# A graph network on one core: the feature block's place in the sum passes, and one signal of TensorE for both

## What is computed

```python
# layer 0, three times:
neigh_mean = segment_sum(h[dst], src, num_segments=n) * inv_deg[:, None]
out = elu(h @ Wg + deg_pos[:, None] * (neigh_mean @ Wl + h @ Ws) + b)
# x = layernorm(x + layer 0)
# layer 1, over the edges in both directions and a loop at each node:
source_node_vec = segment_sum(concat(x[node_i], stf)) / count
neighbors_sum = relu(segment_sum(concat(x[node_j], ef, et) @ W1.T + b1, node_i))
out = concat(neighbors_sum, source_node_vec) @ W2.T + b2
# x = layernorm(x + layer 1)
```

## Time and profile before

| | us |
|---|---|
| median of 3 runs | 10882.93 (10874.25 to 10888.81) |
| the profiled execution | 10844.11 |
| its span | 10842.3 |
| DVE busy | 6451.6 (60%) |
| PE busy, matmuls | 7015.7 (65%) |
| POOL busy | 5221.8 (48%) |
| ACT busy | 3571.9 (33%) |
| sum passes together | 3366 |

### The profile page before, as it was taken

The page is one execution under the profiler, slowest core; times in us unless marked ns, Lnnn a source line. Parts: engine busy times, 40 slices in busy tenths (PEclk is TensorE's granted clock), DMA queues, the critical chain, the costliest instruction groups (busy, mean ns, idle before and its releaser), DMA issues.

```text
span 10842.3 us, 191817 instructions
## 1 busy us (share of the span) xinstructions
PE 7015.7 (65%) x46640; PEld 5921.0 (55%) x46640; DVE 6451.6 (60%) x15194; ACT 3571.9 (33%) x10119; POOL 5221.8 (48%) x4833
## 2 busy tenths in 40 slices
PE   7899981167009999655576665766645566666666
PEld 6688871167008888544444555445544455445556
DVE  8899980022016666544586556865567655675556
ACT  0133320000007777433394112931128511491111
POOL 0058886778654444566304662046620366306660
PEclk9999999999999999777698777987769877897776
DMA  9965555555559999665497665976648866896671
GB/s 385 389 192 143 146 143 139 142 127 126 133 137 308 305 304 301 202 168 166 90 376 269 197 198 111 377 251 195 198 83 338 287 197 197 243 392 193 196 188 28
DMA packets 1567388, 2320.61 MB, mean 214 GB/s; under 512 B 974516, under 2 KB 1046056, under 8 KB 1567320
## 3 DMA queue, kind: packets, MB, share of 16 engines
q1 hardware_dynamic: 1227608, 1356.73, 37.3%
q0 software_dynamic: 292608, 911.36, 30.7%
q10 hardware_dynamic: 47104, 51.75, 2.0%
HBM read 1328.55 MB, written 986.78 MB: 214 GB/s over the span
## 4 chain that ended last, share of the span: by engine, by line
issue 25%; PE 24%; another core or an unknown queue 16%; DVE 14%; ACT 8%; DMA 7%; DVEq 3%; POOL 2%; ACTq 2%; SPq 1%; POOLq 0%
PE ps L759 9%; PE ps L736 4%; DVE mask L1310 3%; ACT ring L1075 3%; PE ps L836 3%; ACT hring L1085 3%; DMA frows<-by_src 2%; PE ps L752 2%; DMA gathered<-ring 2%; DVE ohj L1228 2%; DVE prod L1294 2%; PE ps L747 1%; POOL ring L634 1%; PE ps L674 1%
## 5 line engine op out<-in xcount | busy, mean ns | idle before, releaser
L650 POOL DMA_INDIRECT ring<-gathered,gidx x2176 | 2190.3, 1007 | 3096.1 <-DMA gathered<-ring 1978.2
L580 POOL DMA_INDIRECT by_src<-prow,ppos x1562 | 1949.9, 1248 | 1225.6 <-DMA ppos<-pos 663.8
L836 PE MATMUL ps<-ring,oht_g 128*128 128x192 bf16 x8704 | 1169.5, 286 | 901.7 <-issue 651.0
L1383 DVE TENSOR_REDUCE red<-ps 128x256 f32<-128x768 f32 x680 | 649.9, 956 | 1515.6 <-remote 1010.3
L836 PEld LDWEIGHTS ps<-ring,oht_g 128*128 128x128 bf16 x8704 | 900.4, 124 | 1183.1 <-issue 1049.7
L1463 DVE CAST ring<-ps 128x384 bf16<-128x384 f32 x2176 | 1157.7, 555 | 311.5 <-PE ps L752 227.8
L752 PE MATMUL ps<-hring,oht_g 128*128 128x192 bf16 x8704 | 997.7, 248 | 514.2 <-ACT ring L1075 143.5
L1075 ACT CAST ring<-ps 128x384 bf16<-128x384 f32 x2176 | 1140.9, 527 | 10.9 <-PE ps L752 10.9
L752 PEld LDWEIGHTS ps<-hring,oht_g 128*128 128x128 fp8e4 x8704 | 658.8, 97 | 853.0 <-issue 830.9
L719 PE MATMUL ps<-snap,oht_e 98*128 98x98 f32 x3130 | 1056.8, 441 | 0.0
L1085 ACT COPY hring<-node 128x192 bf16 x2176 | 866.8, 399 | 76.3 <-issue 67.8
(11 more groups left out here) (226 smaller groups left out, 12990.4 us busy)
## 6 DMA issues: line engine op xcount, KB each, us to landing
gathered<-ring SPq DMA_DIRECT2D x544, 768.0 KB
by_src<-zeros SPq DMA_DIRECT2D x34, 6272.0 KB, 45.9
frows<-by_src SPq DMA_DIRECT2D x544, 392.0 KB
oht_g<-oht SPq DMA_DIRECT2D x544, 256.0 KB, 4.8
gathered<-got SPq DMA_DIRECT2D x136, 776.0 KB
prow<-in_edge_attr_n SPq DMA_DIRECT2D x284, 352.0 KB
bc<-tidrow ACTq DMA_DIRECT2D x313, 160.0 KB
prow<-in_edge_attr SPq DMA_DIRECT2D x142, 352.0 KB
```

The lines of the kernel that those rows point to most:

```text
L580: pool.indirect_dma_start(out=table, out_offset=bass.IndirectOffsetOnAxis(ap=ppos[:, s, j:j + 1], axis=0), in_=prow[:, s, j, :], in_offset ...
L650: pool.indirect_dma_start(out=ring[:, c, :], out_offset=None, in_=gb, in_offset=offsets(g, c % 4)).then_inc(q.got[g], 16)
L836: mm = pe.matmul(ps[:, 2 * u + e // 2, e % 2 * 256:e % 2 * 256 + HW], ohq[:, c % 8, :, k], ring[:, c, k * HW:(k + 1) * HW], start=k == 0, ...
L1383: return dve.tensor_reduce(red[:, u, :, 0:D], four_of(bank)[:, :, 0:HW].rearrange("p e (a d) -> p e d a", d=D), AX.X, ALU.add)
```

## The change

TensorE now runs a group's feature block ahead of the group's chunks, and the feature block has no signal of its own: `sum_mm`, set at the last chunk matmul, stands for both. The semaphore `feat_mm` is gone; the sync queue's fetch of block f+2, ScalarE's widening of one-hots and the start of ScalarE's part in the next spread pass wait for `sum_mm` instead. VectorE adds the sum of feature block f in group m itself, with no wait of its own, and no longer adds a last one after the loop.

```diff
--- before.py
+++ after.py
@@ -315,10 +315,10 @@
         feat_row = [sem(f"feat_row{s}") for s in range(2)]
         feat_oh = sem("feat_oh")
         feat_ohf = sem("feat_ohf")
-        feat_mm = sem("feat_mm")
         feat_add = sem("feat_add")
 
         class Sum:
+
 
 
 
@@ -520,7 +520,7 @@
                     for g in range(4):
                         f = 4 * i + (q.f0 + g)
                         if not (last and g > 1):
-                            sp.wait_ge(feat_mm, f + 1)
+                            sp.wait_ge(sum_mm, f + 1)
                             sp.nop(nofuse=True)
                             fetch(f + 2, g % 2)
                 for u in range(2):
@@ -826,6 +826,11 @@
                 def body(i, first):
                     for g in range(4):
                         m, f, u = 4 * i + (q.q0 + g), 4 * i + (q.f0 + g), g % 2
+                        pe.wait_ge(feat_ohf, f + 1)
+                        pe.wait_ge(feat_row[u], 32 * i + (8 * q.f0 + (g // 2 * 16 + 16)))
+                        if q.f0 > 0 or not first:
+                            pe.wait_ge(feat_add, f - 3)
+                        feature_sum(4 + g, fohf[u], frows[:, u])
                         pe.wait_ge(q.oh, m + 1)
                         pe.wait_ge(q.got[g], 64 * i + (q.g0 + 64))
                         if not first or g > 1:
@@ -837,11 +842,6 @@
                                                ring[:, c, k * HW:(k + 1) * HW], start=k == 0, stop=k == K - 1,
                                                skip_group_check=True)
                         mm.then_inc(q.mm, 1)
-                        pe.wait_ge(feat_ohf, f + 1)
-                        pe.wait_ge(feat_row[u], 32 * i + (8 * q.f0 + (g // 2 * 16 + 16)))
-                        if q.f0 > 0 or not first:
-                            pe.wait_ge(feat_add, f - 3)
-                        feature_sum(4 + g, fohf[u], frows[:, u]).then_inc(feat_mm, 1)
                 loop(pe, body)
 
             def layer(q):
@@ -1075,7 +1075,7 @@
                     act.copy(ring[:, c, 0:2 * HW], ps[:, 2 * (c % 4), 0:2 * HW]).then_inc(q.g, 1)
 
                 if q.q0 > 0:
-                    act.wait_ge(feat_mm, q.q0)
+                    act.wait_ge(sum_mm, q.q0)
 
                 def body(i, first):
                     for half in range(2):
@@ -1093,7 +1093,7 @@
                 def whole(f, u, first):
                     act.wait_ge(feat_oh, f + 1)
                     if not first:
-                        act.wait_ge(feat_mm, f - 1)
+                        act.wait_ge(sum_mm, f - 1)
                     act.copy(fohf[u], foh[u][:, :, :].rearrange("p n k -> p k n")).then_inc(feat_ohf, 1)
 
                 def body(i, first, last=False):
@@ -1473,15 +1473,13 @@
                     one_hots(foh[u][:, :, :], 1, f).then_inc(feat_oh, 1)
 
                 def features(f, g, at, first):
-                    dve.wait_ge(feat_mm, f + 1)
                     if not first:
                         dve.wait_ge(feat_add, f)
                     to = node_at(at, F0, FEAT)
                     dve.tensor_tensor(to, to, ps[:, 4 + g, 0:FEAT], ALU.add).then_inc(feat_add, 1)
 
                 def body(i, first, last=False):
-
-                    at_f = tiles(1, q.f0 if first else 4 * i + (q.f0 - 1), 4, mybir.EngineType.DVE)
+                    at_f = tiles(1, 4 * i + q.f0, 4, mybir.EngineType.DVE)
                     for g in range(4):
                         m, f, u = 4 * i + (q.q0 + g), 4 * i + (q.f0 + g), g % 2
                         if u == 0:
@@ -1499,8 +1497,7 @@
                                 dve.wait_ge(q.add, n)
                             to = node_at(at[4 * u + e], A0, D)
                             dve.tensor_tensor(to, to, red[:, u, e, 0:D], ALU.add).then_inc(q.add, 1)
-                        if not first or g > 0:
-                            features(f - 1, (g - 1) % 4, at_f[g - 1 if first else g], q.f0 == 0 and first and g == 1)
+                        features(f, g, at_f[g], q.f0 == 0 and first and g == 0)
                 for m in range(2):
                     ones(m, m)
                     features_ones(q.f0 + m, m, q.f0 == 0)
@@ -1508,8 +1505,6 @@
                 with dve.Fori(1, NI - 1) as i:
                     body(i, False)
                 body(NI - 1, False, True)
-                at_f = tiles(1, q.f0 + NQ - 4, 4, mybir.EngineType.DVE)
-                features(q.f0 + NQ - 1, 3, at_f[3], False)
                 dve.wait_ge(q.add, NB + q.n0)
                 dve.wait_ge(feat_add, q.f0 + NQ)
```

## The result

The changed kernel takes 10927.2 us (median of 22 runs), the kernel before, in 22 runs beside it, 10892.4 us. The ratio is 1.0031, 95% interval 1.0016 to 1.0046: slower by 0.3%, 34 us. Each kernel has some longer executions, which the ratios leave out; the profiles of the changed kernel (11119.8 us) and of b2 further on (11065.0 us) are of such ones, the others are not.

What follows compares the result with a forecast made beforehand. No engine's work reached the middle's 6.03 us a group, so waits were taken to bound it, in the rhythm of TensorE's issue stops. Terms 0 + 0 + 25 + 10 = +35 us, added to 10882.9, gave 10918 us; range 10835 to 11010.

Steps and rivals of the forecast that it cites:

- Step (1): VectorE: one register instruction with a wait less per group, one tile load less per pass; worth 0.
- Step (2): Middle of sum passes: features' waits now stand ahead of the chunks; bounded by -94 and +130 us, taken as 0.
- what would show it: Profile test: middle 6.0 us a group; issue stops shrinking while waits for widened one-hots or rows grow confirms step (2).
- four blocks end at the same time in either order: Middle, TensorE: within 1 us, with the next stop after as many instructions as before; supports taking 0.
- The sign that I named for slower: GpSimd's waits for signals the profile calls remote growing well past 0.5 us a group.
- Step (3): Tail of sum passes: rows requested later; 0.9 us for each of 28 pairs, 25 us, bounds 0 and 70.
- The row that I read: Tail: 8 us without a packet of the fetches' queue, so gathers queued ahead of the request go first.
- Step (4): Pass ends: a third chunk group behind the last waited feature block, one feature add saved; 10 us over four passes.
- longer loop: Rival: feature block inside the signal-to-chunks loop, 118 waits for one-hots each growing 1.1 us; 210 us, 11093, chance 0.15.
- One wait fewer: Rival, middle: rows are there when the one-hots are, feature block fills a pause; -94 + 10, 10799 us, chance 0.21.

Runs made afterwards that it cites:

- b2: Changed kernel with its loop's fetches sent to an unused place and no feature block waiting for rows after the first two; 10906.3 us, ratio to before 1.0046.
- b4: Kernel before with only TensorE's order changed: features ahead of chunks, own feature signal, VectorE's old wait and late add; 10875.4 us, ratio 1.0040.
- d1: b4 plus VectorE making feature one-hots of block f+2 ahead of the wait for group m's matmuls; 10337.7 us against 10368.2 before, ratio 0.9963.
- b1: Kernel before, unchanged, profiled on another chip with late signals; 10848 us, ratio 1.0002.
- b3: Kernel before with its loop's fetches sent to an unused place and no feature block waiting for them; 10877.5 us, ratio 1.0018.
- c1: Changed kernel with feature one-hots of block f+2 made ahead of the wait for group m's matmuls; 10310.5 us against 10347.5 before, ratio 0.9968.
- a1: Changed kernel as it is, run again on a second chip; 10321.9 us against 10358.0 before, ratio 0.9969.
- a2: Changed kernel with a signal of its own behind the feature block, for the fetch and the widening; 10313.3 us, ratio to before 0.9959.
- a3: Changed kernel with features behind the chunks again and the one signal set at the feature block's last matmul; 10299.1 us, ratio to before 0.9944.
- a4: Kernel before with the fetch of block f+2 waiting one chunk group longer, order and signals old; 10361.3 us, ratio 1.0007.

## Why the prediction was right, and where only its sum was

I forecast +35 us and 10918; it is +34 on chip A and 10927, inside the range of 10835 to 11010. The working behind it did not hold in most of its steps, so that the sum came out is luck; on chip B the same sum would have had the wrong sign.

- **Step (1), VectorE, 0: nothing speaks against it.** The order alone (b4) costs 31 us on C where the whole change costs 34 on A, and without the merged add the gain on E (d1) is as large as on B.
- **Step (2), the middle, 0: failed, and this is where the loss is.** The stops did shrink (651 to 115 us) while waits grew, as "what would show it" asked. But that test was too weak: it asked whether stops shrink, not whether waits grow by more, and they did, by 67 us. By the table the middle takes 16.7 us a pass more on A (67 us over four, in the execution of 11119.8 us) and 8.3 in b4 against b1 (33 us, which fits the 31 and 34 us of the medians better). The failed sentence is "four blocks end at the same time in either order": they don't, since TensorE fell into a new rhythm, pairs with a pause. The sign that I named for slower did not help: GpSimd's waits for signals called remote fell (296 to 139 us), while those named after TensorE's chunks rose (205 to 503).
- **Step (3), the tail, 25 us of 0 to 70: oversized.** The table has 1.8 us a pass on A and 1.2 in b4, 5 to 7 us in all. The tail is 104.7 and 103.6 us in the kernel before and 103.3 and 102.6 in b2 and b3, which wait for no rows. So the rows don't set it; with the DMA engines 86 to 90% busy I take it that the gathers do. The row that I read, 8 us without a packet of the fetches' queue, was right about the order of transfers; the price, 1.4 us a gather, charged a wait that didn't bound the tail.
- **Step (4), pass ends, +10 us: wrong sign.** From the last gather to the last feature add it is 3.2 us shorter on A and 2.5 in b4, -10 to -13 us. I had priced what stands behind the last wait for features and not when that wait ends, and what shortens it no run separates.
- The **longer loop**, which I gave 0.15 and 11093 us, named the right place (feature block ahead of the chunks, middle). Its price of 130 us took each of 118 waits at 1.1 us; measured is 33 to 67. With some 240 pauses that is 0.14 to 0.27 us a pause, so most of the 1.1 us of feature one-hots and widening is made up for elsewhere in the loop. That the pauses end with the widening is read from the times (223 of 240 in b4); that a shorter way to the widened one-hots would give the loss back on such a chip is not shown, since c1 and d1 ran on others.
- **One wait fewer** (10799) did not come, on A. On B the changed kernel is faster, for another reason: GpSimd's gathers.

So +35 was 0 + 0 + 25 + 10, and it is about 0 + 33 to 67 + 6 - 12. Errors of opposite sign met. The kind of reading that would have found it: in the earlier trace rows a reduction that waits 1010 us for a signal "that the profile can't tie to a matmul's end" is not a neutral name. In these profiles it goes with signals that come late (it is on A and C, and nowhere on B, D and E), and then the work between a signal and TensorE's next start is what to add up.

## What to carry to other kernels

When an edit puts a block ahead of another on the engine that all others wait for, compare what each needs *after the signal that closes the loop*: here 2.2 us for the chunks, 3.3 for the features. A wait is named by what came last; take it away (b2) before you call it the cause, since another may stand 0.2 us ahead of it. And where two versions are within half a per cent, time them on more than one chip: this change is 0.3% slower on one and 0.3% faster on another. The version with the old order and one signal behind the features gained 0.55% on two chips, and should be timed on a chip like A before it is kept.

## What the runs showed of the hardware

- **Signals of TensorE can come late on some chips.** By the times of the semaphore's updates in the traces, a group's signal `sum_mm` comes 0.01 us after the matmul that sets it in the median on B (a1, a2, a3, a4), and 1.8 us on C (b1; mean 3.2, over 1 us in 332 of 544 groups, with the records of 21 updates missing) and 2.0 on A (before). In the spread passes of the same two profiles TensorE's 2176 signals are not late: the median is 0.01 us and none is over 1 us. So it hangs on the stage too, not on the chip alone. Waits for "remote" stand in a stage far ahead of the sum passes as well: the comparisons of L1330 wait 278.0 us for it on C, and on A 512.5 in the profile of before and 1147.8 in that of the changed kernel. There that execution got long: its next stage starts 205 us later. The time of the same kernel differs by 4.7% (10848 against 10358 us). What delays the signals stays open; no run touched it.
- **A gather that starts beside VectorE's one-hots of chunks takes up to 2.0 us in place of 0.95**, and on the faster chips that is 8 to 10% of GpSimd's busy time in these passes (a1, a3, a4, d1).
- **The clock of the first part doesn't set the time.** The profile's row of granted clocks, first for a1, then for a3:

```profile
PEclk5555555555559999877799887988869988898886
```

```profile
PEclk9999999999999999877799887998878988898886
```

In a1 the first twelve slices, some 3100 us, stand at the level of 1.2 GHz, in a3 at 2.4 GHz. The two executions took 10307.0 and 10307.8 us. They are of two kernels; within one, a1's three executions with a mean granted clock of 0.76 took 10307.0 to 10329.6 us, and its three with 0.91 took 10321.1 to 10333.5.
